# Ternary feed-forward stage: down products a quarter tile later, and the next attention's weights prepared over thirteen tiles

## The chip, the cores and the metric

The kernel runs on one core of one Trainium2 chip. The metric is the device time of one execution in microseconds (us). PE is TensorE, DVE is VectorE, ACT is ScalarE, POOL is GpSimd, SP is SyncE, which here issues all DMAs. The engines run side by side, each through its own list of instructions, and wait for one another by semaphores.

## The reference

Four blocks follow one another on x of 16 x 256 rows of 512: an attention (16 heads) over a context, a feed-forward block with ternary weights, a second attention (8 heads, masked), and a routed feed-forward block. The change is in the second block, where the weights of the third are also made ready:

```
x = x + _L0_xattn_ref(ctx_1024, ctx_1024, _layernorm(x, axis=-1), ...)
x = x + _L0_ffn_ref(_layernorm(x, axis=-1), w_gate, w_up, w_down)
x = x + _L1_xattn_ref(_layernorm(x, axis=-1), ctx_1024, mask, ln_g, ln_b, Wq, Wkv, Wo)
x = x + _L1_ffn_ref(...)

def _act_quant(x):
    scale = 127.0 / jnp.clip(jnp.max(jnp.abs(x), axis=-1, keepdims=True), 1e-05)
    return jnp.clip(jnp.round(x * scale), -128.0, 127.0) / scale
def _bitlinear(x, w):
    return jnp.einsum('bsi,oi->bso', _act_quant(x), _weight_quant(w))
gate = jax.nn.silu(_bitlinear(x, w_gate))       # 512 -> 2048
up = _bitlinear(x, w_up)
return _bitlinear(gate * up, w_down)            # 2048 -> 512
```

In the third block q = (xn * ln_g + ln_b) @ Wq. The rows of Wq are therefore scaled by ln_g once, and ln_b @ Wq becomes a bias column.

## The kernel before

The blocks are phases named a, b, c, m after the prefix of their tiles. Phase b, the ternary stage, takes 4096 rows in 32 tiles of 128. Each engine has a function that writes out its work for one iteration n; `run_elements` writes iterations 0 and 1 out, makes a loop of two iterations a turn for the middle, and writes the last `AHEAD` iterations out again (`AHEAD` = 10: 22 to 31). Only written-out iterations can have work beside them.

A tile goes this way. DVE takes the row statistics (`row_stats`), POOL normalises (`normalise`), DVE finds the largest element and the scales of each row (`x_scale`: `b_xmax`, `b_xs`), POOL rounds to integers in bf16 (`quantise_x`: `b_xn`, `b_xq`), and SP issues a DMA transpose into `b_xqT` (`turn_x`). PE multiplies by gate and up weights in four quarters of 512 columns (`gate_up(el, [c])`: four gate products and four up products each, into two banks per kind). ACT takes the silu of the gate bank (`silus`), DVE multiplies it with the up bank into `b_hid` (line 1562) and takes the largest element of each quarter (`largest`, line 1556). After quarter 3 come the scales of the hidden rows, POOL's rounding in two halves (`quantise_h`), two DMA transposes into `b_hqT` (`turn_h`), 16 down products on PE (`down`, line 1661), and `rows_out` on DVE, whose result SP stores.

In iteration n, PE does all quarters of tile n+1, then down of tile n. DVE does `hidden` of tile n+1, in which `x_scale` of tile n+2 stands behind the product of quarter 1, then what stands beside, then `rows_out` of tile n. SP's queue in iteration n is: x load of tile n+4, `turn_h` half 0 of tile n, residual load of n+1, `turn_h` half 1 of n, `turn_x` of n+2, store of n.

```
wait_apart(sp, hq_ready, el.n * HALVES + half + 1)      # turn_h, L1309
wait_apart(sp, xq_ready, el.n + 1)                      # turn_x, L1304
if cs[0] == 0:                                          # gate_up, PE
    pe.wait_ge(tx_out[el.par], el.dma())
```

Beside iterations 22 to 29 the next attention's weights are made: SP loads the columns and Wq (1 MB) in 22, Wv, Wk, Wo in 23, masks and context in 24; PE computes the query bias in 23 (`query_bias`, 32 thin products of one column, ahead of down), DVE scales Wq's rows in 23 (`gain_weight`), ACT makes high parts in 24 to 27 (`hi_of_weight`), and DVE low parts in 25 to 28 (`lo_of_weight`, one instruction of 128x2048 each).

Of the kernel before, what the change touches and what calls it, by code (L numbers as in the profile page):

```python
# [6 lines left out]
F32 = mybir.dt.float32  # L7
# [138 lines left out]
def attention_phase(nc, ctx, banks, tag, heads, x_in, ctx_in, mask_in, mask_value, x_out, w_views, q_bias, k_bias,  # L146
# [203 lines left out]

    def sync_beside(sp, tile):

        if tile == 22:
            load_columns(sp)
            load_weight(sp, "Wq")
        elif tile == 23:
            for name in MADE[1:]:
                load_weight(sp, name)
        elif tile == 24:
            load_masks(sp)  # L360
            load_first(sp, cbuf[0][:], ctx_in, 0, c_loaded)
        elif tile == 29:
            sp.wait_ge(*prior.gone["x"])
            sp.wait_ge(prior.made["rows"][0], 16)
            sp.wait_ge(prior.made["rows"][1], 16)
            load_first(sp, xbuf[0][:], x_in, 0, x_loaded)
# [104 lines left out]
                                    ALU.mult, ALU.add).then_inc(xn_ready, 1)  # L471

    def gpsimd_beside(pool, tile):
        if tile == 22:
            gpsimd_constants(pool)
        elif tile == 30:
            pool.wait_ge(*prior.gone["xn"])
            normalise(pool, Element(0, 0, batches))
# [69 lines left out]
    def hi_of(act, el, u):  # L548
# [13 lines left out]
        else:  # L562
# [5 lines left out]
            else:  # L568
# [2 lines left out]
                                                ACT.Identity, bias=cols[:, bias, f:f + 1])  # L571
                last.then_inc(hi_done, 1)

    def scalar_beside(act, tile):
        if tile == 23:
            bias_column(act)
        elif 24 <= tile < 28:
            hi_of_weight(act, MADE[tile - 24])

    def scalar_units(act):  # L580

# [100 lines left out]
    def gain_weight(dve):
        n, _, stage, _ = WEIGHTS["Wq"]
        dve.wait_ge(w_loaded[n], 16)
        dve.wait_ge(cols_loaded, NCOLS * 16)
        dve.wait_ge(qbias_mm, 1)
        for k in range(KC):
            rows = stage[:, k * DIM:(k + 1) * DIM]
            nc.vector.tensor_scalar(rows, rows, cols[:, GAIN, k:k + 1], None, ALU.mult).then_inc(w_gained, 1)

    def lo_of_weight(dve, name):
        n, _, stage, w = WEIGHTS[name]
        dve.wait_ge(w_hi, n + 1)
        nc.vector.tensor_tensor(w[:, LO].rearrange("p k n -> p (k n)"), stage,  # L694
                                w[:, HI].rearrange("p k n -> p (k n)").bitcast(F32), ALU.subtract) \
            .then_inc(w_lo, 1)
        if name == "Wq" and normed_twice:
            dve.wait_ge(cols_ready, 1)
        if name == "Wq":
            dve.wait_ge(cols_loaded, NCOLS * 16)  # L700
# [11 lines left out]
    def mask_bias(dve, el):  # L712

        dve.wait_ge(m_loaded[el.par], el.dma())
        nc.vector.tensor_scalar(mbias[:, el.par], mraw[:, el.par], 0.0, mask_value,
                                ALU.is_equal, ALU.mult).then_inc(mbias_ready, 1)
# [38 lines left out]
            last.then_inc(lo_done, 1)  # L755

    def vector_beside(dve, tile):
        if tile == 23:
            gain_weight(dve)
        elif 25 <= tile < 29:  # L760
            lo_of_weight(dve, MADE[tile - 25])
        elif tile == 24:
            mask_bias(dve, Element(0, 0, batches))
        elif tile == 30:
            row_stats(dve, Element(0, 0, batches))
        elif tile == 31:
            for u in PROLOGUE[:7]:
                lo_of(dve, Element(0, 0, batches), u)
# [235 lines left out]

    def tensor_beside(pe, tile):

        if tile == 23:
            query_bias(pe)
        elif tile == 31:
            use(pe, Element(0, 0, batches), "k0")  # L1010
# [112 lines left out]
def ternary_ffn_phase(nc, ctx, banks, tag, x_in, x_out, w_gate, w_up, w_down, prior, tiles=TOK // P):  # L1123
# [163 lines left out]
    gone = {"x": (xn_ready, tiles), "xn": (xq_ready, tiles), "hidden": (h_round, tiles * HALVES), "gates": (h_done, tiles * NC),  # L1287
            "gate bank": (silu_done, tiles * NC), "up bank": (h_done, tiles * NC), "all": (out_done, tiles)}
    made = {"rows": stored}
    AHEAD = 10  # L1290

    def number(el):
        return el.n if isinstance(el.n, int) else None
# [161 lines left out]
    def scalar(act, beside=None):  # L1455
        act.wait_ge(*prior.gone["scores"])
        integer(act, 2, 0)
        integer(act, 2, 1)

        def silus(el, cs):  # L1460
            for c in cs:
                act.wait_ge(g_done, el.n * NC + c + 1)
                wait_for(act, h_done, (el.n - 1) * NC + c + 1)
                if c == 0:
                    act.wait_ge(xs_ready, el.n * 2 + 1)
                nc.scalar.activation(gate[:, c % 4], g_bank[c % 2][:], ACT.Silu, scale=xs[:, el.par, 0:1]) \  # L1466
                    .then_inc(silu_done, 1)

        silus(first[0], range(NC))
        integer(act, 2, 2)  # L1470
        integer(act, 2, 3)

        def iteration(el):
            if el.has(1):
                silus(el.plus(1), range(NC - 1))
            if beside and number(el) == tiles - 1:
                beside.scalar_units(act)
            if el.has(1):
                silus(el.plus(1), range(NC - 1, NC))
# [67 lines left out]
        x_scale(dve, first[0])  # L1547

    def vector(dve, beside=None):
        def hidden(el, steady=True):  # L1550

            wait_for(dve, h_round, (el.n - 1) * HALVES)
            dve.wait_ge(xs_ready, (el.n + 1) * 2)
            def largest(c):
                dve.wait_ge(h_done, el.n * NC + c + 1)
                nc.vector.tensor_reduce(hpart[:, el.par, c:c + 1], hid[:, el.par, c * DIM:(c + 1) * DIM], AX.X,  # L1556
                                        ALU.max, apply_absolute_value=True).then_inc(hpart_ready, 1)

            for c in range(NC):
                dve.wait_ge(u_done, el.n * NC + c + 1)  # L1560
                dve.wait_ge(silu_done, el.n * NC + c + 1)
                nc.vector.scalar_tensor_tensor(hid[:, el.par, c * DIM:(c + 1) * DIM], u_bank[c % 2][:],  # L1562
                                               xs[:, el.par, 1:2], gate[:, c % 4], ALU.mult, ALU.mult) \
                    .then_inc(h_done, 1)
                if c > 0:
                    largest(c - 1)
# [6 lines left out]
            largest(NC - 1)  # L1573
# [64 lines left out]
    def tensor(pe, beside=None):  # L1638
# [1027 lines left out]
```

## Time and profile before

| | us |
|---|---|
| median of 3 runs (lowest to highest) | 2063.67 (2059.59 to 2064.15) |
| the profiled execution, its own time | 2063.06 |
| span of its trace | 2061.3 |
| PE busy | 1949.8 (95%) |
| DVE busy | 1333.8 (65%) |
| ACT busy | 983.5 (48%) |
| POOL busy | 862.7 (42%) |

The ternary stage's products run from about 701 to 1098 us of the span. "Busy" is the sum of an engine's instructions; matmuls overlap, and the end of one is modelled, so that the start of one group to the start of the next is the better measure of PE. In a timeline row stand the start, the time the group took, engine and line, what it writes and reads, how many instructions were merged, and in brackets the idle time before and what ended it. A few matmul records are missing (x15 for 16, for example).

### The profile page before, as it was taken

Reading aid. Unit: us, or ns where it says so; the run is one execution under the profiler, and the core shown is the slowest. Engines: PE = TensorE matmul, PEld = TensorE weight load, DVE = VectorE, ACT = ScalarE, POOL = GpSimd, SP = SyncE. Lnnn points to the kernel's source line nnn. Section 1 sums busy time; section 2 is a strip of 40 time slices with the busy share of each in tenths; the row PEclk is TensorE's granted clock in tenths of the full one; section 3 lists DMA queues with packets and bytes.
Section 4 is the critical chain, followed back from the end, with each engine's and each line's share of the span. In section 5 each row is a group of like instructions: output and inputs, shape, how many; then the busy total and the mean of one; then the engine's idle time right before and its main releaser. Section 6 shows DMA issues by size and latency. Waiting matters only on the chain.

```text
span 2061.3 us, 44849 instructions
## 1 busy us (share of the span) xinstructions
PE 1949.8 (95%) x14010; PEld 1484.8 (72%) x14044; DVE 1333.8 (65%) x4065; ACT 983.5 (48%) x2649; POOL 862.7 (42%) x1501
## 2 busy tenths in 40 slices
PE   5999999999999799998888999999999999999998
PEld 4788888888887444443337888888888876788776
DVE  4777777777776677777774565565555565454475
ACT  3677766767778422222223454444544543222242
POOL 2454545545456667776562212222222213232254
PEclk8999999999999899999998999999999999999999
DMA  5131122122115445556543111212112136232131
GB/s 191 48 126 61 59 92 84 59 69 107 59 56 175 143 116 137 132 130 157 153 110 99 43 43 52 72 41 83 41 51 73 41 114 202 95 102 81 52 133 42
DMA packets 183994, 192.07 MB, mean 93 GB/s; under 512 B 96177, under 2 KB 106417, under 8 KB 183873
## 3 DMA queue, kind: packets, MB, share of 16 engines
q1 hardware_dynamic: 183872, 190.66, 29.7%
q8 instruction: 51, 0.84, 0.2%
q14 instruction: 71, 0.57, 0.1%
HBM read 136.08 MB, written 33.57 MB: 82 GB/s over the span
## 4 chain that ended last, share of the span: by engine, by line
PE 75%; DVE 9%; issue 5%; POOL 4%; DMA 4%; ACT 2%; SPq 0%; POOLq 0%; DVEq 0%; ACTq 0%
PE bank L998 19%; PE bank L987 17%; PE bank L2451 12%; PE bank L1055 7%; PE bank L1068 4%; PE bank L1038 4%; PE bank L1648 4%; DMA b_hqT<-b_hq 3%; PE bank L1661 2%; PE bank L978 2%; POOL b_hround L1406 1%; DVE c_probs L777 1%; DVE b_hpart L1556 1%; POOL b_hq L1411 1%; PE bank L2357 1%
## 5 line engine op out<-in xcount | busy, mean ns | idle before, releaser
L490 POOL TENSOR_SCALAR a_probs<-a_probs,a_rinv 128x256 f32<-128x256 f32 x512 | 238.9, 486 | 282.0 <-DVE a_rinv L793 282.0
L600 ACT ACTIVATE a_probs<-a_probs,a_negm 128x256 f32<-128x256 f32 x512 | 254.6, 502 | 116.8 <-DVE a_negm L777 116.2
L490 POOL TENSOR_SCALAR c_probs<-c_probs,c_rinv 128x256 f32<-128x256 f32 x128 | 67.5, 538 | 396.4 <-DVE c_rinv L793 396.4
L1466 ACT ACTIVATE b_gate<-bank,b_xs 128x512 f32<-128x512 f32 x128 | 87.9, 687 | 276.1 <-PE bank L1648 251.0
L777 DVE CUSTOM_DVE_ANT_0 a_probs<-bank,a_mbias 128x256 f32<-128x256 f32 x512 | 191.8, 418 | 6.3 <-PE bank L1038 4.5
L2451 PE MATMUL bank<-m_xnT,m_s 128*128 128x512 f32 x768 | 187.2, 395 | 2.7 <-DVE m_hid L2192 2.7
L786 DVE COPY a_pT<-bank 128x512 f32<-128x512 f32 x128 | 88.4, 690 | 141.7 <-PE bank L1055 141.6
L600 ACT ACTIVATE c_probs<-c_probs,c_negm 128x256 f32<-128x256 f32 x256 | 127.5, 503 | 90.0 <-DVE c_negm L777 90.0
L1055 PE MATMUL bank<-a_ident,a_probs 128*128 128x128 f32 x1024 | 155.8, 275 | 14.1 <-POOL a_probs L490 7.1
L2451 PEld LDWEIGHTS bank<-m_xnT,m_s 128*128 128x128 f32 x768 | 144.5, 190 | 34.2 <-DVE m_hid L2192 3.1
L1055 PEld LDWEIGHTS bank<-a_ident,a_probs 128*128 128x128 f32 x1024 | 122.4, 142 | 31.8 <-issue 10.5
L1661 PE MATMUL bank<-b_wd,b_hqT 128*128 128x512 bf16 x480 | 117.9, 388 | 25.6 <-DMA b_hqT<-b_hq 24.4
L1648 PE MATMUL bank<-b_wg,b_xqT 128*128 128x512 bf16 x510 | 132.4, 382 | 6.4 <-DMA b_xqT<-b_xq 5.9
L1648 PE MATMUL bank<-b_wu,b_xqT 128*128 128x512 bf16 x512 | 132.8, 382 | 0.0
L1562 DVE SCALAR_TENSOR_TENSOR b_hid<-bank,b_xs,b_gate 128x512 f32<-128x512 f32 x128 | 95.8, 749 | 55.5 <-PE bank L1648 38.2
L1981 POOL TENSOR_TENSOR m_hidT<-m_hid,m_hidT 128x512 fp32r<-128x512 f32 x32 | 41.8, 1307 | 195.8 <-ACT m_hidT L2062 195.8
L1661 PEld LDWEIGHTS bank<-b_wd,b_hqT 128*128 128x128 bf16 x512 | 48.6, 99 | 90.6 <-issue 26.5
L998 PE MATMUL bank<-a_cT,a_wk 128*128 128x256 f32 x768 | 109.4, 293 | 3.9 <-DVE a_wq L694 3.9
L987 PE MATMUL bank<-a_wv,a_cT 128*128 128x512 f32 x384 | 105.6, 412 | 7.1 <-DVE a_cT L741 7.1
L998 PEld LDWEIGHTS bank<-c_cT,c_wk 128*128 128x128 f32 x768 | 93.9, 191 | 23.2 <-DVE c_xnT L741 17.2
L998 PE MATMUL bank<-c_cT,c_wk 128*128 128x256 f32 x768 | 100.3, 287 | 10.4 <-DVE c_xnT L741 10.4
L608 ACT ACTIVATE a_pT<-bank 128x512 f32<-128x512 f32 x128 | 76.4, 597 | 70.6 <-PE bank L1055 69.9
(279 smaller groups left out, 4487.2 us busy)
## 6 DMA issues: line engine op xcount, KB each, us to landing
m_ew<-in_L_ffn_w_dram SPq DMA_DIRECT2D x24, 512.0 KB, 8.1
a_cbuf<-in_ctx_dram SPq DMA_DIRECT2D x16, 512.0 KB, 5.9
a_xbuf<-in_x_dram SPq DMA_DIRECT2D x16, 512.0 KB, 5.3
a_resb<-in_x_dram SPq DMA_DIRECT2D x16, 512.0 KB, 3.9
x<-a_resb SPq DMA_DIRECT2D x16, 512.0 KB, 2.8
b_xbuf<-x SPq DMA_DIRECT2D x32, 256.0 KB, 2.8
b_resb<-x SPq DMA_DIRECT2D x32, 256.0 KB, 3.0
x<-b_resb SPq DMA_DIRECT2D x32, 256.0 KB, 2.0
```

What stands on the lines that cost most here:

```text
L490: last = nc.gpsimd.tensor_scalar(pr, pr, rinv[:, s, r:r + 1], 0.0, ALU.mult, ALU.add)
L600: nc.scalar.activation(pr, pr, ACT.Exp, bias=negm[:, s, h % 2, t:t + 1], scale=-1.0, accum_out=ssum[:, s, QT * (h % 2) + t:QT * (h % 2) + ...
L777: nc.vector.tensor_tensor_reduce(out=probs[:, s, h % 2, t], in0=s_bank[h][:, t * SEQ:(t + 1) * SEQ], in1=mbias[:, el.par], scale=-sm_scale ...
L786: nc.vector.tensor_copy(pT[:, (h // hpg) % 2, h % hpg].rearrange("p t n -> p (t n)"), pt_bank[:]) \
L987: last = nc.tensor.matmul(dst[:], src[:, a, k, t * P:(t + 1) * P], w[:, b, k], start=(k == 0 and (a, b) == TERMS[0]), stop=(k == KC - 1 an ...
L998: last = nc.tensor.matmul(dst[:, m * SEQ:(m + 1) * SEQ], w[:, b, k, f * P:(f + 1) * P], src[:, a, k], start=(k == 0 and (a, b) == TERMS[0] ...
L1055: last = nc.tensor.transpose(pt_bank[:, kt * SEQ + t * P:kt * SEQ + (t + 1) * P], probs[:, s, m, t, kt * P:(kt + 1) * P], ident[:])
L1466: nc.scalar.activation(gate[:, c % 4], g_bank[c % 2][:], ACT.Silu, scale=xs[:, el.par, 0:1]) \
L1562: nc.vector.scalar_tensor_tensor(hid[:, el.par, c * DIM:(c + 1) * DIM], u_bank[c % 2][:], xs[:, el.par, 1:2], gate[:, c % 4], ALU.mult, AL ...
L1648: last = nc.tensor.matmul(bank[c % 2][:], xqT[:, el.par, k], w[:, k, c * DIM:(c + 1) * DIM], start=(k == 0), stop=(k == KC - 1))
L1661: last = nc.tensor.matmul(d_bank[:], hqT[:, el.par, k], wd[:, k], start=(k == 0), stop=(k == IK - 1))
L2451: ins = nc.tensor.matmul(bank[:], *operands(a, b, k), start=(k == 0 and (a, b) == TERMS[0]), stop=(k == KC - 1 and (a, b) == TERMS[-1]))
```

## The change

1. Order of all engines in the ternary stage. Quarter 0 of a tile is taken out of its place at the head of its tile and put behind quarter 3 of the tile before. On PE iteration n now is: quarters 1, 2, 3 of tile n+1, quarter 0 of tile n+2, down of tile n. ACT's silus and DVE's products follow that order; DVE's product of quarter 0 stands ahead of the work beside and of `rows_out`. SP's and POOL's order is as before.
2. The work for the next attention's weights begins four tiles earlier and is spread over tiles 18 to 30: loads in 18 to 20, constants on POOL in 18, query bias on PE and its copy on ACT in 20, high parts in 22 to 25. `AHEAD` goes from 10 to 14, so that iterations 18 to 31 are written out.
3. The rows of Wq are scaled on ACT (four activations of 128x512 in tile 21) instead of DVE (four in 23).
4. Low parts are made in halves of 128x1024, one in each of tiles 22 to 29, instead of whole in 25 to 28.

```
@@ sync_beside @@
-        if tile == 22:
+        if tile == 18:
             load_columns(sp)
             load_weight(sp, "Wq")
-        elif tile == 23:
+        elif tile == 19:
...
-        elif tile == 24:
+        elif tile == 20:
             load_masks(sp)
@@ scalar_beside, and gain_weight now here @@
+    def gain_weight(act):
...
+        for k in range(KC):
+            rows = stage[:, k * DIM:(k + 1) * DIM]
+            nc.scalar.activation(rows, rows, ACT.Identity, scale=cols[:, GAIN, k:k + 1]).then_inc(w_gained, 1)
-        if tile == 23:
+        if tile == 20:
             bias_column(act)
-        elif 24 <= tile < 28:
-            hi_of_weight(act, MADE[tile - 24])
+        elif tile == 21:
+            gain_weight(act)
+        elif 22 <= tile < 26:
+            hi_of_weight(act, MADE[tile - 22])
@@ vector_beside @@
-        if tile == 23:
-            gain_weight(dve)
-        elif 25 <= tile < 29:
-            lo_of_weight(dve, MADE[tile - 25])
-        elif tile == 24:
+        if tile == 21:
             mask_bias(dve, Element(0, 0, batches))
+        elif 22 <= tile < 30:
+            lo_of_weight(dve, MADE[(tile - 22) // 2], (tile - 22) % 2)
@@ tensor_beside @@
-        if tile == 23:
+        if tile == 20:
             query_bias(pe)
@@ ternary phase @@
-    AHEAD = 10
+    AHEAD = 14
@@ scalar @@
         silus(first[0], range(NC))
+        silus(first[1], [0])
...
             if el.has(1):
-                silus(el.plus(1), range(NC - 1))
+                silus(el.plus(1), range(1, NC))
+            if el.has(2):
+                silus(el.plus(2), [0])
@@ vector: hidden @@
-            for c in range(NC):
...
+            for c in range(1, NC):
+                product(el, c)
+                largest(el, c - 1)
...
                 if steady and c == 1 and el.has(1):
                     x_scale(dve, el.plus(1))
@@ vector: iteration @@
             if el.has(1):
                 hidden(el.plus(1))
+            if el.has(2):
+                product(el.plus(2), 0)
@@ tensor @@
             elif el.has(1):
-                gate_up(el.plus(1), range(NC - 1))
+                gate_up(el.plus(1), range(1, NC))
+            if el.has(2):
+                gate_up(el.plus(2), [0])
             if beside and number(el) == tiles - 1:
                 beside.tensor_units(pe)
-            if el.has(1):
-                gate_up(el.plus(1), range(NC - 1, NC))
             down(el, beside)
```

PE before, from quarter 3 of tile 1 on in iteration 0. `b_tx_out0` is the transpose of tile 2's input, `b_th_out00` and `b_th_out10` are those of tile 0's hidden rows:

```order
L1648 MATMUL bank<-b_wg,b_xqT 128x512 [waits b_silu_done]
L1648 MATMUL bank<-b_wg,b_xqT 128x512 x3
L1648 MATMUL bank<-b_wu,b_xqT 128x512 [waits b_h_done]
L1648 MATMUL bank<-b_wu,b_xqT 128x512 x3
L1661 MATMUL bank<-b_wd,b_hqT 128x512 [waits b_th_out00,b_w_out]
L1661 MATMUL bank<-b_wd,b_hqT 128x512 x7
L1661 MATMUL bank<-b_wd,b_hqT 128x512 [waits b_th_out10]
L1661 MATMUL bank<-b_wd,b_hqT 128x512 x7
L1648 MATMUL bank<-b_wg,b_xqT 128x512 [waits b_silu_done,b_tx_out0]
L1648 MATMUL bank<-b_wg,b_xqT 128x512 x3
```

The same place on PE now:

```order
L1659 MATMUL bank<-b_wg,b_xqT 128x512 [waits b_silu_done]
L1659 MATMUL bank<-b_wg,b_xqT 128x512 x3
L1659 MATMUL bank<-b_wu,b_xqT 128x512 [waits b_h_done]
L1659 MATMUL bank<-b_wu,b_xqT 128x512 x3
L1659 MATMUL bank<-b_wg,b_xqT 128x512 [waits b_silu_done,b_tx_out0]
L1659 MATMUL bank<-b_wg,b_xqT 128x512 x3
L1659 MATMUL bank<-b_wu,b_xqT 128x512 [waits b_h_done]
L1659 MATMUL bank<-b_wu,b_xqT 128x512 x3
L1672 MATMUL bank<-b_wd,b_hqT 128x512 [waits b_th_out00,b_w_out]
L1672 MATMUL bank<-b_wd,b_hqT 128x512 x7
L1672 MATMUL bank<-b_wd,b_hqT 128x512 [waits b_th_out10]
```

The wait for `b_tx_out0` now stands ahead of down and not behind it, and so in every later iteration.

DVE before, in the loop, from `rows_out` to `x_scale`:

```order
L1585 SCALAR_TENSOR_TENSOR b_resb<-bank,b_hs,b_resb 128x512 [waits b_d_done,b_hs_ready,b_r_loaded0]
L32 REGISTER_ALU
L1553 REGISTER_ALU [waits b_h_round]
L1560 REGISTER_ALU [waits b_xs_ready]
L1562 SCALAR_TENSOR_TENSOR b_hid<-bank,b_xs,b_gate 128x512 [waits b_silu_done,b_u_done]
L1560 REGISTER_ALU
L1562 SCALAR_TENSOR_TENSOR b_hid<-bank,b_xs,b_gate 128x512 [waits b_silu_done,b_u_done]
L1556 TENSOR_REDUCE b_hpart<-b_hid 128x1 [waits b_h_done]
L1520 TENSOR_REDUCE b_xmax<-b_xn 128x1 [waits b_x_round,b_xn_ready]
```

And now:

```order
L1557 REGISTER_ALU [waits b_h_round]
L1558 REGISTER_ALU [waits b_xs_ready]
L1560 SCALAR_TENSOR_TENSOR b_hid<-bank,b_xs,b_gate 128x512 [waits b_silu_done,b_u_done]
L1589 ISA
L1592 SCALAR_TENSOR_TENSOR b_resb<-bank,b_hs,b_resb 128x512 [waits b_d_done,b_hs_ready,b_r_loaded0]
L1558 REGISTER_ALU
L1560 SCALAR_TENSOR_TENSOR b_hid<-bank,b_xs,b_gate 128x512 [waits b_silu_done,b_u_done]
L1566 TENSOR_REDUCE b_hpart<-b_hid 128x1 [waits b_h_done]
L1524 TENSOR_REDUCE b_xmax<-b_xn 128x1 [waits b_x_round,b_xn_ready]
```

The product of quarter 0 went ahead of `rows_out`; the largest element of x (`b_xmax`) still stands behind the product of quarter 1.

SP, the end of the loop and the first iteration written out behind it, now:

```order
L1308 DMA_TRANSPOSE b_xqT<-b_xq 128x4x128 [waits b_xq_ready]
L38 REGISTER_ALU
L1337 DMA x<-b_resb 128x512 [waits b_out_done]
L66 REGISTER_ALU
L66 COMPARE_AND_BRANCH
L338 DMA c_cols<-in_L_xattn_ln_g_dram 128x4x1
L338 DMA c_cols<-in_L_xattn_ln_b_dram 128x4x1
L332 DMA c_raw_wq<-in_L_xattn_Wq_dram 128x4x512
L1241 DMA b_xbuf<-x 128x512 [waits b_xn_ready]
L1313 DMA_TRANSPOSE b_hqT<-b_hq 128x8x128 [waits b_d_done,b_hq_ready]
L1303 DMA b_resb<-x 128x512 [waits b_stored1]
L1313 DMA_TRANSPOSE b_hqT<-b_hq 128x8x128 [waits b_d_done,b_hq_ready]
```

Before, the same rows stood there; but the loop ended four iterations later.

## Rows read from the trace of the kernel before

**Rows 1.** The page: shares of the chain, costliest groups (busy, mean ns, idle before).

```profile
PE 75%; DVE 9%; issue 5%; POOL 4%; DMA 4%; ACT 2%; SPq 0%; POOLq 0%; DVEq 0%; ACTq 0%
...
L1661 PE MATMUL bank<-b_wd,b_hqT 128*128 128x512 bf16 x480 | 117.9, 388 | 25.6 <-DMA b_hqT<-b_hq 24.4
L1648 PE MATMUL bank<-b_wg,b_xqT 128*128 128x512 bf16 x510 | 132.4, 382 | 6.4 <-DMA b_xqT<-b_xq 5.9
```

**Rows 2.** Timeline of PE: start, us, line; first group of iterations 1, 10, 22, 25, 30.

```profile
729.65 1.03 PE L1648 MATMUL bank<-b_wg,b_xqT 128*128 128x512 bf16 x4
...
819.23 1.03 PE L1648 MATMUL bank<-b_wg,b_xqT 128*128 128x512 bf16 x4
...
822.70 1.89 PE L1661 MATMUL bank<-b_wd,b_hqT 128*128 128x512 bf16 x8
...
826.63 1.03 PE L1648 MATMUL bank<-b_wg,b_xqT 128*128 128x512 bf16 x4
...
955.84 1.03 PE L1648 MATMUL bank<-b_wg,b_xqT 128*128 128x512 bf16 x4
...
1005.92 1.03 PE L1648 MATMUL bank<-b_wg,b_xqT 128*128 128x512 bf16 x4
...
1064.94 1.03 PE L1648 MATMUL bank<-b_wg,b_xqT 128*128 128x512 bf16 x4
```

**Rows 3.** Timeline of DVE, POOL and SP's queue in iteration 9.

```profile
819.44 0.75 DVE L1562 SCALAR_TENSOR_TENSOR b_hid<-bank,b_xs,b_gate 128x512 f32<-128x512 f32 x1 [0.87 <-PE bank L1648]
...
822.07 0.70 POOL L1394 TENSOR_SCALAR b_xn<-b_xn,b_xmax 128x512 f32<-128x512 f32 x1 [0.70 <-DVE b_xmax L1233]
...
823.68 1.19 SPq L1305 DMA_TRANSPOSE b_xqT<-b_xq  x1
```

**Rows 4.** The tile b_xqT: its transposes, from issue to landing.

```profile
DMA to landing us min/median/max: 2.4/2.5/3.5
```

**Rows 5.** The chain of waits: from b_hqT's landing to the next down product.

```profile
824.85 0.27 issue
```

**Rows 6.** Timeline of SP's queue: a store, and the transpose of x behind it.

```profile
1055.74 0.34 SPq L1334 DMA_DIRECT2D x<-b_resb  x1
...
1061.21 1.19 SPq L1305 DMA_TRANSPOSE b_xqT<-b_xq  x1
```

**Rows 7.** The same view in iterations 22, 23 and 24.

```profile
957.04 0.36 SPq L1334 DMA_DIRECT2D x<-b_resb  x1
...
965.85 1.19 SPq L1305 DMA_TRANSPOSE b_xqT<-b_xq  x1
973.15 0.35 SPq L1334 DMA_DIRECT2D x<-b_resb  x1
...
985.76 1.19 SPq L1305 DMA_TRANSPOSE b_xqT<-b_xq  x1
993.33 0.35 SPq L1334 DMA_DIRECT2D x<-b_resb  x1
...
1001.45 1.19 SPq L1305 DMA_TRANSPOSE b_xqT<-b_xq  x1
```

**Rows 8.** Timeline of PE: query bias, and down behind gaps of two lengths.

```profile
966.88 5.30 PE L1661 MATMUL bank<-b_wd,b_hqT 128*128 128x512 bf16 x15 [3.97 <-DMA b_hqT<-b_hq]
...
978.92 3.63 PE L937 MATMUL bank<-c_cols,c_raw_wq 128*128 128x1 f32 x32
...
1002.47 3.61 PE L1661 MATMUL bank<-b_wd,b_hqT 128*128 128x512 bf16 x15 [3.21 <-DMA b_hqT<-b_hq]
```

**Rows 9.** Windows of PE: window, length, busy, granted clock, DMA share, GB/s.

```profile
967.00:967.50 0.50, 0.50 (x2) 0.50 1.28 290
```

**Rows 10.** Groups of 955 to 1075 us by form, DVE and ACT.

```profile
L689 DVE TENSOR_SCALAR c_raw_wq<-c_raw_wq,c_cols 128x512 f32<-128x512 f32 x4 | 4.3, 1126 | 0.0
...
L694 DVE TENSOR_TENSOR c_wq<-c_raw_wq,c_wq 128x2048 fp32r<-128x2048 f32 x1 | 2.3, 2279 | 0.0
...
L1466 ACT ACTIVATE b_gate<-bank,b_xs 128x512 f32<-128x512 f32 x36 | 24.7, 687 | 84.3 <-PE bank L1648 78.1 <-issue 6.2
```

More of the change, by code:

```diff
@@ L473, in gpsimd_beside @@
     def gpsimd_beside(pool, tile):
-        if tile == 22:
+        if tile == 18:
             gpsimd_constants(pool)
@@ L572, in hi_of @@
                 last.then_inc(hi_done, 1)
+    def gain_weight(act):
+        n, _, stage, _ = WEIGHTS["Wq"]
+        act.wait_ge(w_loaded[n], 16)
+        act.wait_ge(cols_loaded, NCOLS * 16)
+        act.wait_ge(qbias_mm, 1)
+        for k in range(KC):
+            rows = stage[:, k * DIM:(k + 1) * DIM]
+            nc.scalar.activation(rows, rows, ACT.Identity, scale=cols[:, GAIN, k:k + 1]).then_inc(w_gained, 1)
     def scalar_beside(act, tile):
-        if tile == 23:
+        if tile == 20:
             bias_column(act)
-        elif 24 <= tile < 28:
-            hi_of_weight(act, MADE[tile - 24])
+        elif tile == 21:
+            gain_weight(act)
+        elif 22 <= tile < 26:
+            hi_of_weight(act, MADE[tile - 22])
     def scalar_units(act):
@@ L680, in scalar, with lo_of_weight @@
         attn_hi(Element(0, batches - 1, batches), GROUPS - 1)
[L682 to L691, printed above, removed]
+    def lo_of_weight(dve, name, half=None):
         n, _, stage, w = WEIGHTS[name]
+        hi, lo = (w[:, part].rearrange("p k n -> p (k n)") for part in (HI, LO))
+        cut = slice(0, KC * DIM) if half is None else slice(half * KC * DIM // 2, (half + 1) * KC * DIM // 2)
         dve.wait_ge(w_hi, n + 1)
-        nc.vector.tensor_tensor(w[:, LO].rearrange("p k n -> p (k n)"), stage,
-                                w[:, HI].rearrange("p k n -> p (k n)").bitcast(F32), ALU.subtract) \
-            .then_inc(w_lo, 1)
+        last = nc.vector.tensor_tensor(lo[:, cut], stage[:, cut], hi[:, cut].bitcast(F32), ALU.subtract)
+        if half == 0:
+            return
+        last.then_inc(w_lo, 1)
         if name == "Wq" and normed_twice:
@@ L1474, in iteration @@
             if el.has(1):
-                silus(el.plus(1), range(NC - 1))
+                silus(el.plus(1), range(1, NC))
+            if el.has(2):
+                silus(el.plus(2), [0])
             if beside and number(el) == tiles - 1:
                 beside.scalar_units(act)
-            if el.has(1):
-                silus(el.plus(1), range(NC - 1, NC))
             if beside and number(el):
@@ L1549, in vector, with product, largest @@
     def vector(dve, beside=None):
-        def hidden(el, steady=True):
[L1552 to L1557, printed above, removed]
-            for c in range(NC):
[L1560 to L1566, printed above, removed]
+        def product(el, c):
+            if c == 0:
+                wait_for(dve, h_round, (el.n - 1) * HALVES)
+                dve.wait_ge(xs_ready, (el.n + 1) * 2)
+            dve.wait_ge(u_done, el.n * NC + c + 1)
+            dve.wait_ge(silu_done, el.n * NC + c + 1)
+            nc.vector.scalar_tensor_tensor(hid[:, el.par, c * DIM:(c + 1) * DIM], u_bank[c % 2][:],
+                                           xs[:, el.par, 1:2], gate[:, c % 4], ALU.mult, ALU.mult) \
+                .then_inc(h_done, 1)
+        def largest(el, c):
+            dve.wait_ge(h_done, el.n * NC + c + 1)
+            nc.vector.tensor_reduce(hpart[:, el.par, c:c + 1], hid[:, el.par, c * DIM:(c + 1) * DIM], AX.X,
+                                    ALU.max, apply_absolute_value=True).then_inc(hpart_ready, 1)
+        def hidden(el, steady=True):
+            for c in range(1, NC):
+                product(el, c)
+                largest(el, c - 1)
                 if isinstance(el.n, int) and el.n == 1 and c in (1, 2):
@@ L1572, in hidden @@
                     row_stats(dve, el.plus(2))
-            largest(NC - 1)
+            largest(el, NC - 1)
             dve.wait_ge(hpart_ready, (el.n + 1) * NC)
@@ L1591, in vector @@
         row_stats(dve, first[2])
+        product(first[0], 0)
         hidden(first[0], steady=False)
+        product(first[1], 0)
         def iteration(el):
@@ L1666, in tensor @@
         gate_up(first[0], range(NC))
+        gate_up(first[1], [0])
         def iteration(el):
             if isinstance(el.n, int) and el.n == 0:
-                gate_up(el.plus(1), [0, 1])
+                gate_up(el.plus(1), [1])
                 turn(pe, range(4 * HALF, 5 * HALF))
@@ L1673, in iteration @@
                 turn(pe, range(5 * HALF, 6 * HALF))
+                gate_up(el.plus(1), [3])
             elif el.has(1):
-                gate_up(el.plus(1), range(NC - 1))
+                gate_up(el.plus(1), range(1, NC))
+            if el.has(2):
+                gate_up(el.plus(2), [0])
             if beside and number(el) == tiles - 1:
                 beside.tensor_units(pe)
-            if el.has(1):
-                gate_up(el.plus(1), range(NC - 1, NC))
             down(el, beside)
```

## The prediction

> **What bounds the kernel now.** I read the page's chain of work first. Three quarters of it is PE [rows 1], so what makes PE wait in a stage is what a change of that stage is worth. Of PE's groups in the ternary stage, the down products (L1661) waited 25.6 us, 24.4 of it for the DMA transposes b_hqT; the gate products (L1648) waited 5.9 us for b_xqT, all of it at the stage's start [rows 1].
>
> Then PE's timeline. The stage repeats one tile per iteration: four quarters of gate and up, then down. Two quarters take 822.70 - 819.23 = 3.47 us, and down with its waits 826.63 - 822.70 = 3.93 us [rows 2]. Without waits a tile is six such quarter lengths (16 of its 48 products are down's), 10.4 us. Iterations 1 to 21 take (955.84 - 729.65) / 21 = 10.77 us each, 22 to 24 together 1005.92 - 955.84 = 50.1 us, and 25 to 29 together 1064.94 - 1005.92 = 59.0 us [rows 2]. So iterations 1 to 21 are within 4% of PE's own work. The three slow ones are those beside which the next attention's weights load.
>
> The third view decides the case: how the next tile's input gets to PE. In iteration n DVE takes the product of quarter 1 of tile n+1 (819.44), then the largest element of its quarter 0, then the scale of tile n+2's rows; POOL rounds them (822.07), and SP issues their transpose b_xqT at 823.68 [rows 3]. It lands 2.5 us later in the median [rows 4], at 826.2, and PE starts 0.27 us behind a landing [rows 5]: 826.45. Tile n+2's first gate product runs at 826.63 [rows 2]. That is only 0.2 us later: the transpose is in time because the 3.5 us of down stand between.
>
> **The change part by part.**
>
> *Order of PE.* Quarter 0 of tile n+2 now stands ahead of down n, so it is wanted at 822.70 instead of 826.63. Nothing brings its input earlier: the row scale is still made behind the product of quarter 1 on DVE (the order shows it), that product needs PE's quarter 1, and x's transpose is still the last of three in SP's queue. Chain of the data, from the start of quarter 2: 823.68 - 819.23 = 4.45, + 2.5 + 0.27 = 7.22 us. PE arrives after 3.47. It waits 3.75 us in each of iterations 1 to 29. The delay feeds itself back: quarter 1 of the next tile starts only when this quarter 0 and down are through, so nothing catches up. Period: 10.4 + 3.75 = 14.2 us.
>
> The second chain to the same transpose is SP's queue: down, rows out, store, x load, two transposes of h, transpose of x. The store is issued 957.04 - 955.84 = 1.20 us behind the end of down [rows 2, 7], and from store to transpose of x the queue takes 5.47 us where it is nearly unbroken (1055.74 to 1061.21) [rows 6], some of it waiting for POOL. Period by this chain: 1.20 + 5.47 + 2.77 (landing and start) + 1.73 (quarter 0) + 3.5 (down) = 14.7 us, an upper bound. I take 14.35 inside the loop and 14.15 where the code is written out, since there SP has no loop registers to set.
>
> What goes: down n gets 12.1 instead of 10.4 us from quarter 3 of its tile, so the waits for b_hqT end. They are inside the 10.77 that I subtract, so they are credited.
>
> *Iterations without loads.* Loop, 1 to 17: 17 x (14.35 - 10.77) = +60.9. Written out, 21 to 29: 9 x 14.15 = 127.4, against iterations 18 to 21 (4 x 10.77 = 43.1) and 25 to 29 (59.0) of before: +25.3.
>
> *Iterations with loads.* They are now 18 to 20 and the same DMAs stand in the same places of the queue. From store to transpose of x they took 965.85 - 957.04 = 8.8, 985.76 - 973.15 = 12.6 and 1001.45 - 993.33 = 8.1 us [rows 7]. SP's chain is now the period, with 9.2 us around it as above (1.20 + 2.77 + 1.73 + 3.5): 18.0, 21.8 and 17.3. The query bias products (3.6 us) [rows 8] stand between quarter 0 and down of iteration 20, where nothing hides them: +3.6, and 0.5 for the wait on ACT's copy. Then the clock. After an idle 3.97 us the granted clock was 0.50, the lower of the two levels (1.2 GHz), and down took 5.30 us instead of 3.62 [rows 8, 9]: +1.7. These gaps are 8 to 11 us long, so I add it once in each and once more in iteration 20, behind the thin bias products. Sum 57.1 + 4.1 + 6.8 = 68.0 against 50.1: +17.9.
>
> *The clock elsewhere.* After an idle 3.21 us the down products still ran at full clock (3.61 us); after 3.97 they did not [rows 8]. The new wait, seen as 3.6 us of idle, lies between. Bounds: 0, and 26 x 1.68 = 44 us. I take it nearer to the first, a fall in about two of 26, +3.5. The Trainium skill ("TensorE: Matmul & The Clock Gate", HAM oscillation) says the opposite of what I take: a kernel that waits on a DMA before each burst of matmuls restarts every burst throttled. By that the sum would have the 44 us; the trace agrees for 3.97 and not for 3.21.
>
> *Work moved to ACT, halves on DVE.* Row scaling leaves DVE (4.3 us for four) and costs ACT four activations of 128x512, by its own of that size 4 x 0.69 = 2.8 us [rows 10], behind the last activation of quarter 0 and so beside down and the next wait. Low parts of 2.28 us become two of about 1.14 [rows 10], ahead of rows out and inside the 3.5 us of down. Both 0. In the kernel before, the whole ones delayed rows out, the store and the transposes behind it, which is why iterations 25 to 29 took 11.8 each: that gain is credited above. If the cover were gone, the worst is 2.8 once and 8 x 1.14 = 9 us. Loads, constants and masks four tiles earlier: 0 beyond the above. Iterations 0, 30 and 31: 0. In iteration 0 the transposes of weights give the input time, and 31 starts as before. I bound these at -3 to +3.
>
> Sum: 60.9 + 25.3 + 17.9 + 3.5 = +107.6. The profiled execution took 2063.06 us, within 0.6 of the median of the runs, so 2063.1 + 107.6 = **2170.7 us**.
>
> **The rivals.**
>
> A. *The clock falls in every new gap.* For: 3.6 is no farther from 3.97 than from 3.21. Against: the idle 3.21 us were ridden out, and a fall needs the gap to be long enough in each iteration, not in one. 2170.7 - 3.5 + 44 = 2211 us. The loaded iterations have it already. The Trainium skill's rule above speaks for this rival.
>
> B. *The change does what it says: x's transpose is in time and only the waits for h go.* It ends on the other side. Place: PE ahead of quarter 0. It decides when x's transpose is issued by 822.70 - 2.77 = 819.93, which is 3.75 us before it now is. For: 24.4 us of waits for b_hqT are there to be had [rows 1]; two slowed downs would add 3.4. Against: the issue at 823.68 [rows 3], and that the scale's place on DVE is not moved. 2063 - 28 = 2035 us.
>
> C. *Only half a wait per tile.* With PE later, POOL and SP are free when the data come, and transposes meet less traffic. For: POOL's wait before rounding varied, so parts of the 4.45 us may give way. Against: each of its pieces starts when its predecessor ends, and nothing but the landing depends on traffic. 26 x 1.9 less: 2121 us.
>
> **How the numbers follow.** My forecast 0.74 (its own range 2148 to 2192: the period 13.9 to 14.6 in 26 iterations, the loaded ones 8 us either way), A 0.13, B 0.07, C 0.06. Predicted is the likeliest, 2171. The range 2145 to 2212 leaves out B, C and the tail of A. About 0.2% is what a measurement of this kernel can tell from no change. Faster 0.07, within 0.2% 0.01 (no case sits there), slower 0.92.
>
> **What would show it.** In the changed profile the gate products must wait for DMA b_xqT some 29 times, above 100 us in all and about 3.6 us each in the loop, and the down products for b_hqT almost never outside iterations 18 to 20. PE's iterations should be 14.2 to 14.5 us apart. The gap between SP's transpose of x and PE's quarter 0 should be 2.8 us, and between quarter 2's start and that transpose 4.4 to 4.8. The granted clock should stay at 1.0 over most of the loop; 0.5 behind every gap is rival A. Iterations still 10.5 us apart is B and makes all of this wrong.

## The result: 7.7% slower, and the profile after

The changed kernel took 2222.68 us in the median of 4 runs (2220.60 to 2226.01), the kernel before 2063.91 us in its 4 (2059.59 to 2065.46). The ratio is 1.0774, with an interval of 1.0752 to 1.0797. Forecast were 2171 us in a range of 2145 to 2212, so the direction is right, the size is 52 us short, and the time lies 11 us above the range. The profiled execution took 2220.6 us.

The page of the kernel after, in the order of [rows 1]: busy times, granted clock in 40 slices, shares of the chain, and the two groups of products.

```profile
PE 2004.1 (90%) x14011; PEld 1499.8 (68%) x14044; DVE 1328.2 (60%) x4065; ACT 985.2 (44%) x2653; POOL 855.3 (39%) x1501
PEclk8999999999999878877799899999999999999999
PE 76%; DVE 8%; issue 5%; SPq 4%; DMA 4%; ACT 2%; POOL 2%; DVEq 0%; POOLq 0%; ACTq 0%
...
L1659 PE MATMUL bank<-b_wg,b_xqT 128*128 128x512 bf16 x507 | 150.4, 424 | 127.9 <-DMA b_xqT<-b_xq 127.5
L1672 PE MATMUL bank<-b_wd,b_hqT 128*128 128x512 bf16 x493 | 135.2, 431 | 3.4 <-issue 2.0
```

Two things stand beside [rows 1]. The wait has changed its name: the down products had waited 24.4 us for b_hqT, now it is the gate products that wait 127.5 us for b_xqT. And the products themselves grew longer: 424 ns for 382, and 431 for 388. PE is busy 54 us more with the same work. The clock row dips in slices 14 to 20, which is the ternary stage.

PE's waits of that stage (690 to 1290 us; total, number, longest):

```profile
PE bank L1659 <- DMA b_xqT<-b_xq: 127.5, 30, 11.4
...
PE bank L1672 <- DMA b_hqT<-b_hq: 0.3, 1, 0.3
```

PE's timeline, the view of [rows 2]: iterations 1, 13 and 14, the query bias of iteration 20, and iteration 22, one of those written out.

```profile
743.15 1.04 PE L1659 MATMUL bank<-b_wg,b_xqT 128*128 128x512 bf16 x4 [3.32 <-DMA b_xqT<-b_xq]
...
943.53 1.89 PE L1659 MATMUL bank<-b_wg,b_xqT 128*128 128x512 bf16 x4 [3.53 <-DMA b_xqT<-b_xq]
945.21 1.91 PE L1659 MATMUL bank<-b_wu,b_xqT 128*128 128x512 bf16 x4
947.34 4.43 PE L1672 MATMUL bank<-b_wd,b_hqT 128*128 128x512 bf16 x15 [0.22 <-issue]
951.61 1.03 PE L1659 MATMUL bank<-b_wg,b_xqT 128*128 128x512 bf16 x4
...
960.82 1.89 PE L1659 MATMUL bank<-b_wg,b_xqT 128*128 128x512 bf16 x4 [3.87 <-DMA b_xqT<-b_xq]
...
1081.21 6.83 PE L940 MATMUL bank<-c_cols,c_raw_wq 128*128 128x1 f32 x32
...
1118.17 1.04 PE L1659 MATMUL bank<-b_wg,b_xqT 128*128 128x512 bf16 x4 [3.34 <-DMA b_xqT<-b_xq]
...
1119.91 3.62 PE L1672 MATMUL bank<-b_wd,b_hqT 128*128 128x512 bf16 x15
```

The idle time in brackets is the predicted one (3.3 to 3.9 us). What follows it is not: at 943.53 four gate products take 1.89 us instead of 1.03. From there quarter 0 takes 3.81 us (943.53 to 947.34) where it takes 1.73 at full clock, and down 4.27 (947.34 to 951.61) where it takes 3.46 (from 1119.91 to the next product at 1123.37). One fall costs 2.9 us here, and in the next iteration 2.8.

Windows of PE, columns as in [rows 9]: that fall, the products behind it, and the stretch from quarter 0 of iteration 5 to that of iteration 17.

```profile
944.00:948.00 4.00, 3.78 (x10) 0.50 0.00 0
948.00:952.00 4.00, 4.00 (x16) 0.82 0.00 0
952.00:956.00 4.00, 4.00 (x20) 1.00 0.39 130
807.00:1011.00 204.00, 157.51 (x564) 0.80 0.34 85
```

The mean granted clock is 0.80 over these 204 us, and in PE's timeline quarter 0 runs at half clock in each of iterations 3 to 17 (in iteration 2 its up products do). Two falls in 26 iterations had been forecast.

From one down's end to the next, iteration 1 took 13.85 us, 2 took 15.88, and 3 to 17 took 16.9 to 17.2. The sums, in us:

| iterations | before | forecast | after |
|---|---|---|---|
| 1 to 17 | 183.2 | 244.0 | 285.4 |
| 18 to 20 (after: 21.0, 24.1, 29.0) | 32.0 | 68.0 | 74.1 |
| 21 to 29 | 120.1 | 127.4 | 134.9 |
| together | 335.3 | 439.4, and 3.5 for the clock | 494.4 |

The difference after less before is 159.1, against 157.6 in the spans. Ahead of and behind these iterations 1.5 us came back, within the 3 that were allowed.

What sets the wait in the loop is read from the chain of waits, from the end of one down to the next quarter 0:

```profile
951.91 0.76 DVE b_resb L1592
952.80 0.35 SPq L1337
...
953.87 0.34 SPq L1241
...
954.53 1.24 SPq L1313
...
956.13 0.33 SPq L1303
...
956.69 1.23 SPq L1313
...
958.24 2.45 DMA b_xqT<-b_xq
960.69 0.13 issue
960.82 2.74 PE bank L1659 x6
```

It is SP's queue: store (L1337), load of x, transpose of h, load of the residual, transpose of h, transpose of x. Quarter 2 starts at 953.33, so x's transpose is issued 4.91 us behind that start and PE begins 7.49 us behind it. The data were ready a little sooner, by the timeline of DVE and POOL, the rows that answer to [rows 3]:

```profile
953.55 0.75 DVE L1560 SCALAR_TENSOR_TENSOR b_hid<-bank,b_xs,b_gate 128x512 f32<-128x512 f32 x1 [0.89 <-PE bank L1659]
...
956.17 0.69 POOL L1397 TENSOR_SCALAR b_xn<-b_xn,b_xmax 128x512 f32<-128x512 f32 x1 [7.25 <-DVE b_xmax L1236]
...
957.16 0.62 POOL L1402 TENSOR_SCALAR b_xq<-b_xn 128x512 bf16<-128x512 f32 x1 [0.29 <-POOL b_xn L1397]
```

POOL has rounded x at 957.78, and SP issues the transpose at 958.24.

### The profile page after: what moved, and what is told of

The parts are those of the page before. It is cut to its first block, busy times and chain, and to the rows that moved or that the text cites. A ratio compares the mean times of both kernels' runs of the same rounds, so it can differ in the third digit from the quotient of the medians.

```text
span 2218.9 us, 44672 instructions
## 1 busy us (share of the span) xinstructions
PE 2004.1 (90%) x14011; PEld 1499.8 (68%) x14044; DVE 1328.2 (60%) x4065; ACT 985.2 (44%) x2653; POOL 855.3 (39%) x1501
## 4 chain that ended last, share of the span: by engine, by line
PE 76%; DVE 8%; issue 5%; SPq 4%; DMA 4%; ACT 2%; POOL 2%; DVEq 0%; POOLq 0%; ACTq 0%
PE bank L1001 17%; PE bank L990 16%; PE bank L2464 11%; PE bank L1058 7%; PE bank L1659 6%; PE bank L1672 6%; PE bank L1071 4%; PE bank L1041 4%; DMA b_xqT<-b_xq 4%; SPq L1313 3%; PE bank L981 2%; DVE c_probs L780 1%; DVE b_resb L1592 1%; PE bank L2370 1%; DVE c_pT L789 0%
## 5 line engine op out<-in xcount | busy, mean ns | idle before, releaser
L1659 PE MATMUL bank<-b_wg,b_xqT 128*128 128x512 bf16 x507 | 150.4, 424 | 127.9 <-DMA b_xqT<-b_xq 127.5
L2464 PE MATMUL bank<-m_xnT,m_s 128*128 128x512 f32 x768 | 185.1, 392 | 2.7 <-DVE m_hid L2205 2.7
L1659 PEld LDWEIGHTS bank<-b_wg,b_xqT 128*128 128x128 bf16 x512 | 50.6, 104 | 201.8 <-issue 86.0
L611 ACT ACTIVATE c_probs<-c_probs,c_negm 128x256 f32<-128x256 f32 x256 | 127.4, 503 | 90.0 <-DVE c_negm L780 90.0
L1659 PE MATMUL bank<-b_wu,b_xqT 128*128 128x512 bf16 x503 | 151.5, 425 | 1.8 <-issue 1.8
L1672 PE MATMUL bank<-b_wd,b_hqT 128*128 128x512 bf16 x493 | 135.2, 431 | 3.4 <-issue 2.0
L1672 PEld LDWEIGHTS bank<-b_wd,b_hqT 128*128 128x128 bf16 x512 | 57.5, 113 | 85.3 <-issue 43.4
L1001 PE MATMUL bank<-c_cT,c_wk 128*128 128x256 f32 x768 | 100.3, 287 | 10.4 <-DVE c_xnT L746 10.4
L1001 PEld LDWEIGHTS bank<-c_cT,c_wk 128*128 128x128 f32 x768 | 93.9, 191 | 23.2 <-DVE c_xnT L746 17.2
```

The lines of the kernel that those rows point to most:

```text
L611: nc.scalar.activation(pr, pr, ACT.Exp, bias=negm[:, s, h % 2, t:t + 1], scale=-1.0, accum_out=ssum[:, s, QT * (h % 2) + t:QT * (h % 2) + ...
L1001: last = nc.tensor.matmul(dst[:, m * SEQ:(m + 1) * SEQ], w[:, b, k, f * P:(f + 1) * P], src[:, a, k], start=(k == 0 and (a, b) == TERMS[0] ...
L1659: last = nc.tensor.matmul(bank[c % 2][:], xqT[:, el.par, k], w[:, k, c * DIM:(c + 1) * DIM], start=(k == 0), stop=(k == KC - 1))
L1672: last = nc.tensor.matmul(d_bank[:], hqT[:, el.par, k], wd[:, k], start=(k == 0), stop=(k == IK - 1))
L2464: ins = nc.tensor.matmul(bank[:], *operands(a, b, k), start=(k == 0 and (a, b) == TERMS[0]), stop=(k == KC - 1 and (a, b) == TERMS[-1]))
```

## The experiments

Two theories of the 159 us. Theory 1: the wait for x's transpose is all of it, once as idle time and once as the clock that falls behind the idle time. In form 1a SP's queue is what comes last in the loop, in form 1b the chain of the data. Theory 2, the rival: a good part lies elsewhere, in the work for the next attention's weights, in DVE's order or in contention of the transposes. Each ratio is against the runs of before on the same chip.

### w_only: the order as before, everything else of the change

```
             elif el.has(1):
-                gate_up(el.plus(1), range(1, NC))
-            if el.has(2):
-                gate_up(el.plus(2), [0])
+                gate_up(el.plus(1), range(NC - 1))
...
+            if el.has(1):
+                gate_up(el.plus(1), range(NC - 1, NC))
             down(el, beside)      # silus and hidden likewise
```

> Quarter order as before, everything else of the change kept (weights over 13 tiles, row scaling on ACT, halves of low parts, AHEAD 14). Theory 1: all the loss comes from the order. Then this kernel is at or below before: the waits of iterations 25 to 29 (59.0 - 5 x 10.77 = 5.2 us) mostly go, the three loaded iterations stay as they were: 2055 to 2061 us. Rival: the earlier loads or the scaling on ACT cost something of their own: above 2068 us.

2066.01 us, ratio 1.0002 (0.9987 to 1.0018): no change. The time lies between the two ranges given. The other three parts of the change don't make the loss. The gain expected of the spread weights didn't come: iterations 18 to 20 took 54.8 us (before's loaded ones 50.1), 25 to 29 took 57.9 for 59.0.

### o_only: the order alone, on the kernel before

> Kernel before with the new quarter order alone (weights as before in 22 to 29, AHEAD 10). Theory 1: it has the whole loss, 2222 to 2235 us, and PE waits about 125 us for b_xqT. Rival: order and earlier loads act together, and the order alone costs clearly less, under 2200 us.

2234.25 us, ratio 1.0828 (1.0792 to 1.0864), with 129.0 us of waits for b_xqT in 30 places. By both runs the weights have no part in the loss. DVE's order is a part of what this run moves, so that it can't tell it apart; `both` below keeps the product of quarter 0 ahead of `rows_out` and has no loss. Against contention speaks that the transposes of x landed no later after than before (2.4/2.5/3.5 us at the least, in the median and at the most in both traces). The run is 12 us dearer than the whole change (iterations 1 to 29: 506.5 us for 494.3). Some 8 of these are iterations 18 to 21, here still in the loop at 68.3 us together, where the whole change has four more written-out ones (15.0 us each in its iterations 21 to 29); this is a sum of rows, no run isolates it.

### fill14: products that nobody reads, in the wait

```
             if el.has(2):
+                if not (isinstance(el.n, int) and el.n == 0):
+                    for _ in range(14):
+                        nc.tensor.matmul(banks[1][:], wd[:, 0, 0:P], wd[:, 0], start=True, stop=True)
                 gate_up(el.plus(2), [0])
```

> Changed kernel, with 14 products more on PE (128x512, into a bank nobody reads) ahead of quarter 0's wait in iterations 1 to 29: 3.0 us of PE work inside the gap of 3.5 us. It computes the same output. Theory 1: the granted clock stays at 1.0 in the loop, an iteration takes 13.9 to 14.2 us instead of 17.05, and the time falls by 50 to 60 us to 2162 to 2172 us, although PE has 89 us more to do. Rival: the iteration's 17 us do not come from the clock; then the time stays at 2220 or rises.

2172.14 us, ratio 1.0527 (1.0490 to 1.0564). Its timeline and its clock (window of 200 us):

```profile
908.76 3.19 PE L1692 MATMUL bank<-b_wd 128*128 128x512 bf16 x14
...
912.45 1.03 PE L1659 MATMUL bank<-b_wg,b_xqT 128*128 128x512 bf16 x4 [0.50 <-DMA b_xqT<-b_xq]
```

```profile
800.00:1000.00 200.00, 185.96 (x840) 0.98 0.42 101
```

PE does 3.19 us more work per iteration and the kernel is 50 us faster than the one after. The transpose comes about as late as it did (PE starts quarter 0 at 912.45, 7.14 us behind the start of quarter 2, for 7.49); what changed is that the clock stays up. Iterations 1 to 17 took 242.4 us in all, 14.26 each, against 285.4 with the falls: 43.0 us for the clock there. The forecast had 14.35 for an iteration without a fall.

### fill5: a third as many

> As fill14 with 5 products, 1.1 us: the gap keeps 2.4 us of idle. Theory 1: a gap that much shorter is ridden out, the granted clock stays at 1.0 in the loop, an iteration takes 14.2 to 14.4 us, and the time is that of fill14 within 8 us, 2164 to 2180 us. Rival: the clock goes by PE's share of work over an iteration; then it falls here still, and the time is 2190 to 2220 us.

2185.10 us, ratio 1.0590 (1.0568 to 1.0613), between what the two theories gave. The idle time left is 2.2 to 3.0 us in the loop, yet the clock still fell in six of iterations 1 to 17 (15.6 to 16.3 us each, the others 14.0 to 14.5), and not behind the longer gaps only:

```profile
787.48 1.03 PE L1659 MATMUL bank<-b_wg,b_xqT 128*128 128x512 bf16 x4 [2.85 <-DMA b_xqT<-b_xq]
...
789.21 3.62 PE L1672 MATMUL bank<-b_wd,b_hqT 128*128 128x512 bf16 x16
...
846.37 1.03 PE L1659 MATMUL bank<-b_wg,b_xqT 128*128 128x512 bf16 x4 [2.86 <-DMA b_xqT<-b_xq]
847.24 1.49 PE L1659 MATMUL bank<-b_wu,b_xqT 128*128 128x512 bf16 x4
848.52 4.89 PE L1672 MATMUL bank<-b_wd,b_hqT 128*128 128x512 bf16 x16
```

Behind an idle 2.85 us nothing falls. Behind 2.86 the clock falls in the middle of the up products (1.49 us for 1.03), and down takes 4.89 for 3.62.

### xs_early: the row scale ahead of the product of quarter 1

```
         def hidden(el, steady=True):
+            if steady and el.has(1):
+                x_scale(dve, el.plus(1))
             for c in range(1, NC):
                 product(el, c)
                 largest(el, c - 1)
-                if steady and c == 1 and el.has(1):
-                    x_scale(dve, el.plus(1))
```

> Changed kernel, with DVE's row scale of the next input ahead of the product of quarter 1 instead of behind it, so that data for x's transpose are ready some 2 us earlier. Theory 1a (SP's queue is the chain that binds, as the chain of waits after shows): iterations stay at 17 us, 2215 to 2225 us. Rival 1b (the data chain binds): each gap shortens by 1.5 to 2 us, the clock stays up, and the time falls to 2110 to 2140 us.

2212.46 us, ratio 1.0722 (1.0686 to 1.0759), 3 us below the range of theory 1a. POOL had x rounded at 955.38 (954.76 + 0.62), SP issued its transpose only at 958.07, and the loop didn't move: iterations 1 to 17 took 285.6 us. The written-out ones gained, 127.8 for 134.9, four of nine at 13.1 to 13.3. So SP's queue comes last in the loop (1a), the data where the code is written out.

### sp_late: store and residual load behind the transposes

```
         SP: load_x, turn_h half 0, turn_h half 1, turn_x,
+            store(n - 1), load_res
-            store(n)        (load_res stood between the halves)
```

> Changed kernel, SP's queue alone reordered: the store of tile n-1 and the residual load of n+1 stand behind the transposes of iteration n, so that x's transpose no longer waits in the queue for rows out of the tile before. Theory 1a (in the loop the queue binds, 4.91 us from quarter 2 to the transpose's issue, where the data need 4.45): the loop's gaps shorten by 0.4 us, less than the clock needs, 2205 to 2222 us. Rival: the queue is the whole matter, and with it gone the wait for b_xqT falls under 60 us and the time under 2150 us.

2199.03 us, ratio 1.0658 (1.0636 to 1.0680), below what was expected. The chain of waits now runs through the data, as in the written-out part before: DVE's x scale, POOL (below), the transpose.

```profile
881.98 0.70 POOL b_xn L1402
...
882.96 0.63 POOL b_xq L1407
...
883.65 2.46 DMA b_xqT<-b_xq
886.12 0.13 issue
886.25 3.59 PE bank L1664 x8
```

The idle time is 3.4 to 3.5 us, and the loop fell to 274.4 us, 11.0 less. The two chains end within some 0.4 us of each other, so neither helps much there alone. The larger part of this run's 24 us lies elsewhere: iterations 18 to 20 took 60.0 us for 74.1, and PE's idle time in them was 3.3, 6.6 and 3.3 us for 8.1, 11.4 and 7.5.

### both: both chains shortened

```
DVE   hidden(n+1), product(n+2, 0)
+     x_scale(n+3)
POOL  -quantise_x(n+2), normalise, quantise_h both halves
      +normalise, quantise_h half 0, quantise_x(n+3), quantise_h half 1
SP    +load_x, turn_h half 0, turn_x, store(n-1), turn_h half 1, load_res
```

> Changed kernel with the input of quarter 0 made in time: x's row scale on DVE right behind the product of quarter 0 of the tile before last's iteration, POOL rounds x between the two halves of the hidden rows, SP issues x's transpose between the two of h, and the store behind it. Theory 1 (the only fault of the change is that quarter 0's input comes behind it): the gap of 3.5 us shrinks to 0 to 0.5 us, iterations take 10.4 to 11.0 us, the time is 2045 to 2070 us. Rival: POOL, with 9.2 us of work a tile in a fixed order, or the hidden rows' second half, now 1.4 us later, becomes the wait, iterations stay above 11.5 us and the time above 2085 us.

2044.53 us, ratio 0.9915 (0.9897 to 0.9934), 0.9% faster than the kernel before and 0.5 us below the range of theory 1. The timeline of all engines in one iteration:

```profile
868.36 0.62 POOL L1407 TENSOR_SCALAR b_xq<-b_xn 128x512 bf16<-128x512 f32 x1 [0.29 <-POOL b_xn L1402]
...
869.05 1.19 SPq L1308 DMA_TRANSPOSE b_xqT<-b_xq  x1
...
871.86 1.03 PE L1670 MATMUL bank<-b_wg,b_xqT 128*128 128x512 bf16 x4
...
873.58 3.62 PE L1683 MATMUL bank<-b_wd,b_hqT 128*128 128x512 bf16 x16
```

x's transpose is issued at 869.05 and wanted at 871.86: 2.81 us for a landing of 2.5 and a start of 0.13. No product waits here, and 16 of iterations 1 to 17 take 10.35 to 10.37 us, which is PE's own work (10.4 in the forecast).

### both_nopool: as both, but x behind both halves of h on POOL and SP

> As the kernel both, but POOL rounds x behind both halves of the hidden rows, and SP issues x's transpose behind both of h. DVE's early scale is kept. Theory 1, from the rows: POOL ends the hidden rows 9.1 us after quarter 3 and x at 10.6; the transpose lands at 13.2, PE wants it at 10.4. A gap of 2.5 to 2.9 us comes back in each iteration, it is short enough that the granted clock falls in some iterations only, and the time is 2110 to 2150 us. Rival: POOL's order does not matter once DVE makes the scale early; the time stays within 10 us of both (2044).

2081.64 us, ratio 1.0087 (1.0054 to 1.0119). The waits for b_xqT are 40.1 us in 22 places, and iterations alternate between some 12.1 and 10.8. Both numbers I had given missed: the place in POOL's and SP's order is worth 37 us, about half of what the sum of the instructions gave, because only every second iteration has a wait of any size (1.7 us at 854.78).

### old_order_fix: both's early x with before's order of quarters

> As the kernel both, but with the quarter order of before (down behind quarter 3, not behind the next quarter 0). Theory 1: down then wants h's second half 12.1 us after quarter 3, which with x's rounding in between lands at 14.2: a wait of about 2 us per iteration for b_hqT, 2085 to 2125 us. That would show that a down product a quarter later is worth something once x is in time. Rival: the gain of both comes from the early x alone and the quarter order is worth nothing: 2040 to 2055 us.

2055.96 us, ratio 0.9963 (0.9951 to 0.9976), far below the range of theory 1 and 1 us above the rival's. The wait for b_hqT was 20.7 us in all and not 2 in each iteration. Here x is early and down stands where it stood before. PE's waits, of this kernel and of `both`:

```profile
PE bank L1675 <- DMA b_hqT<-b_hq: 20.7, 23, 4.7
```

```profile
PE bank L1670 <- DMA b_xqT<-b_xq: 13.1, 7, 5.2
...
PE bank L1683 <- DMA b_hqT<-b_hq: 1.6, 2, 1.0
```

The rival, by which the order is worth nothing once x is in time, is out too: the later down is worth some 11 us (2056.0 to 2044.5, on two chips, the intervals of the ratios apart; iterations 1 to 29 took 331.6 and 319.7).

### both_spread: and one weight per iteration

```
+        elif tile in (21, 22):
+            load_weight(sp, MADE[tile - 19])
...
-            for name in MADE[1:]:
-                load_weight(sp, name)
+            load_weight(sp, MADE[1])
```

> As the kernel both, with one weight load of 1 MB per iteration: Wq in 18, Wv in 19, Wk in 21, Wo in 22 (both has three in 19, an iteration of 18.4 us where 18 with one load takes 11.3). Theory: 19 falls to about 11.5, 21 and 22 rise by about 1 us each, sum 5 to 7 us less than both, 2037 to 2040 us. Rival: the transposes pay for every byte of weights wherever it stands in the queue; then the sum does not change, 2042 to 2048 us.

2040.44 us, ratio 0.9876 (0.9846 to 0.9907), the lowest median of all; but its interval overlaps that of `both`, so by the times alone the two are not told apart. In the trace they are: three weights of 1 MB no longer stand together ahead of a transpose: iterations 18 to 20 took 11.39, 10.36 and 14.26 us, 36.0 together for 45.7 in `both`, and 21 and 22 did not grow (10.36 each). Iteration 30's down starts 7.7 us earlier than in `both` (1048.51 for 1056.19), but only 2.5 of it show in the span. 3.7 us of it went in the products of the fourth block, which nothing touched (187.3 for 185.1 us, 96.2 for 94.7, with the same waits); why they differ is open, and the kernel before had 187.2 for the first of them. One of its four runs took 2033.34 us.

## Why the prediction was right and where it failed

*Order of PE* was right. The predicted wait was 3.75 us, seen as 3.6 idle, in iterations 1 to 29. Measured were 3.3 to 4.2 without loads, mostly 3.3 to 3.9; with those of iterations 0 and 18 to 20 the waits are 30, 127.5 us in all. An iteration without a fall took 14.26 us in the loop of `fill14` and 13.85 to 14.1 written out, for 14.35 and 14.15. *The second chain* was given as an upper bound of 14.7. It is in fact what comes last in the loop (7.49 us behind quarter 2 instead of 7.22), and the data chain in the written-out part. `xs_early` and `sp_late` show it from both sides.

*The clock elsewhere* is the step that failed: "a fall in about two of 26, +3.5". It failed twice. The number: I took one gap that had been ridden out, 3.21 us, and one that had not, 3.97 [rows 8], for the ends of a threshold, and placed 3.6 between them. In the loop the clock fell at each gap from iteration 2 on. And the price: I took the 1.68 us of [rows 8] for what any fall costs. There the clock was back up before down ended, for the quarter behind that down, from the same timeline of the kernel before, runs at full clock:

```profile
972.02 1.03 PE L1648 MATMUL bank<-b_wg,b_xqT 128*128 128x512 bf16 x4
```

In the loop of the kernel after it stayed low through quarter 0 (2.08 us more) and into down (0.81 more), 2.9 us in all. That is no fixed price either: of the written-out iterations, 21, 24 and 25 had a fall and took 15.2 to 15.7 us for 13.9, 1.3 to 1.8 more. What decides how long the clock stays low is open. Rival A, with every gap a fall, used the same 1.68 and came to 2211, still 12 us short. With 43.0 in the loop by `fill14`, its mechanism was the true one there; I had given it 0.13. The rule of the Trainium skill that the prediction weighed and set aside ("TensorE: Matmul & The Clock Gate", HAM oscillation: bursts behind a DMA wait each restart throttled) agrees with the loop of this trace, iterations 3 to 17, and not with its written-out iterations, of which four of nine had no fall.

*Iterations with loads* came to 74.1 us for 68.0. Their waits were about right (8.1, 11.4 and 7.5 us of idle time, forecast as 8 to 11). What was missing is in the main the clock again: quarter 0 at half in each, and the query bias, costed at full clock with 3.6 us [rows 8], took 6.8 behind the fall.

*Iterations 21 to 29* came to 134.9 for 127.4, since five of nine had a fall.

*Work moved to ACT, halves on DVE* cost nothing, as forecast: four activations took 2.55 us (2.8), the halves 1.2 to 1.9 (1.14), and `w_only` is level with before. The gain that I credited there for iterations 25 to 29 was small, 1.1 us.

The sum: the forecast's 439.4 + 3.5 = 442.9 us for iterations 1 to 29 against 494.4. The missing 51.5 is 41.4 in the loop, 6.1 in the loaded iterations and 7.5 in 21 to 29, less the 3.5. `fill14` took 50.5 us back by keeping the clock up, and lands at 2172 where the forecast without falls would be 2167.

## What to carry to other kernels

Before moving work ahead of what it used to stand behind, look up how early its input is ready: here down was the cover of x's transpose, which had 0.2 us to spare. An input that is needed a step earlier has to be made a step earlier on each engine of its chain, DVE, POOL and SP's queue together; DVE's part alone gave 10 us of the 159 and SP's alone 24 (14 of them in the three loaded iterations), the three together gave all of it and some 18 more. And where a new wait of the length seen here (3.3 to 3.9 us) repeats in a PE loop, work out the time with a clock fall at each one, at the 1.3 to 2.9 us that one cost here, before taking the milder case.

## What the runs showed of the hardware

The length of the idle time does not tell whether the clock falls. The pair of `fill5` above shows it, and in `sp_late` the clock fell at the first of two gaps of the same length and not at the second, where down starts 1.73 us behind quarter 0 for 3.05:

```profile
1108.01 1.89 PE L1664 MATMUL bank<-b_wg,b_xqT 128*128 128x512 bf16 x4 [3.35 <-DMA b_xqT<-b_xq]
...
1111.06 3.62 PE L1677 MATMUL bank<-b_wd,b_hqT 128*128 128x512 bf16 x16
...
1184.23 1.04 PE L1664 MATMUL bank<-b_wg,b_xqT 128*128 128x512 bf16 x4 [3.35 <-DMA b_xqT<-b_xq]
...
1185.96 3.62 PE L1677 MATMUL bank<-b_wd,b_hqT 128*128 128x512 bf16 x16
```

The first pair of rows also shows a fall that was over before down began: it cost 1.3 us, less than half of one in the loop of the kernel after. In `fill5` falls were seen at idle times from 2.2 us on, and in the kernel after gaps of up to 3.4 us (3.38 in iteration 23) had none. What decides between them stays open; no run here isolates it. Fourteen products, 3.19 us together, in a gap of 3.7 us kept the mean granted clock at 0.98 for 0.80 and made a kernel that has more products to do 50 us faster.
